# Transposing the softmax tiles of two units in every second step, with one copy out of PSUM for both and six buffers

## What is computed

```python
q = (queries @ Wq).reshape(b, s, KV_HEADS, GROUP, HEAD_DIM)   # 8 key heads x 4 query heads, 32 wide
k = (keys @ Wk).reshape(b, s, KV_HEADS, HEAD_DIM)
v = (values @ Wv).reshape(b, s, KV_HEADS, HEAD_DIM)
scores = jnp.einsum('bqhgd,bkhd->bhgqk', q, k) * scale
attn = jax.nn.softmax(scores, axis=-1)
out = jnp.einsum('bhgqk,bkhd->bqhgd', attn, v)
...
x = x + jnp.tanh(g_xattn[0]) * _L0_xattn_ref(_layernorm(x, axis=-1), ctx_4096, ctx_4096, L0_xattn_Wq, L0_xattn_Wk, L0_xattn_Wv, L0_xattn_Wo)
x = x + jnp.tanh(g_ffn[0]) * _L0_ffn_ref(_layernorm(x, axis=-1), L0_ffn_W_gate, L0_ffn_W_up, L0_ffn_W_down)
```

## Time and profile before

| | |
|---|---|
| time, median of 3 runs | 1900.26 us (1899.02 to 1903.03) |
| the profiled execution's own time | 1900.98 us |
| its span in the profile | 1899.2 us |
| PE busy | 1887.4 us (99%) |
| DVE busy | 1235.0 us (65%) |
| ACT busy | 825.8 us (43%) |
| POOL busy | 866.5 us (46%) |

### The profile page before, as it was taken

The page is one execution under the profiler, slowest core; times in us unless marked ns, Lnnn a source line. Parts: engine busy times, 40 slices in busy tenths (PEclk is TensorE's granted clock), DMA queues, the critical chain, the costliest instruction groups (busy, mean ns, idle before and its releaser), DMA issues.

```text
span 1899.2 us, 27364 instructions
## 1 busy us (share of the span) xinstructions
PE 1887.4 (99%) x9346; PEld 1555.7 (82%) x9346; DVE 1235.0 (65%) x1716; ACT 825.8 (43%) x1947; POOL 866.5 (46%) x632
## 2 busy tenths in 40 slices
PE   9999999999999999999999999999999999999999
PEld 7888888888888788888888788888888888888887
DVE  7877887787787855555554767665555555546565
ACT  5863773683584533333332444443333333333333
POOL 1430440251255598888887311116666766630000
PEclk9999999999999999999999999999999999999999
DMA  6335326326324345354536876752323232267675
GB/s 212 90 130 172 104 65 246 98 62 233 119 79 172 118 143 186 138 193 147 181 140 216 301 242 205 243 177 75 120 101 110 84 118 103 89 212 251 213 227 182
DMA packets 127196, 298.78 MB, mean 157 GB/s; under 512 B 12672, under 2 KB 24448, under 8 KB 121728
## 3 DMA queue, kind: packets, MB, share of 16 engines
q1 hardware_dynamic: 126960, 297.45, 46.3%
q10 hardware_dynamic: 144, 0.13, 0.0%
HBM read 221.25 MB, written 71.57 MB: 154 GB/s over the span
## 4 chain that ended last, share of the span: by engine, by line
PE 95%; DMA 2%; POOL 2%; DVE 1%; issue 0%; ACT 0%; SPq 0%; POOLq 0%; DVEq 0%; ACTq 0%
PE ps L1592 28%; PE ps L1594 28%; PE ps L1593 28%; PE ps L1642 3%; PE ps L1633 2%; PE ps L1653 2%; PE ps L1634 2%; PE ps L1804 1%; DMA raw<-ws 1%; PE ps L1690 1%; PE ps L1815 1%; DMA ws<-dw 1%; DMA kv_raw<-in_wc 0%; DMA dw<-in_wd 0%; DVE bl L1160 0%
## 5 line engine op out<-in xcount | busy, mean ns | idle before, releaser
L1592 PE MATMUL ps<-xop_h,w_h 128*128 128x512 f32 x1208 | 471.8, 391 | 0.0
L1594 PE MATMUL ps<-xop_h,w_l 128*128 128x512 f32 x1208 | 470.1, 389 | 0.0
L1593 PE MATMUL ps<-xop_l,w_h 128*128 128x512 f32 x1208 | 470.0, 389 | 0.0
L1160 DVE TENSOR_TENSOR bl<-raw,bh 128x1024 fp32r<-128x1024 f32 x154 | 199.5, 1304 | 143.1 <-ACT bh L862 142.8
L1594 PEld LDWEIGHTS ps<-xop_h,w_l 128*128 128x128 f32 x1208 | 226.7, 188 | 47.1
L1592 PEld LDWEIGHTS ps<-xop_h,w_h 128*128 128x128 f32 x1208 | 226.8, 188 | 46.6 <-DVE cc L1405 0.3
L1593 PEld LDWEIGHTS ps<-xop_l,w_h 128*128 128x128 f32 x1208 | 226.8, 188 | 46.4
L862 ACT ACTIVATE bh<-raw 128x1024 fp32r<-128x1024 f32 x154 | 163.0, 1061 | 225.9 <-PE ps L1594 195.9
L1160 DVE TENSOR_TENSOR w_l<-fraw,w_h 128x512 fp32r<-128x512 f32 x130 | 135.4, 1042 | 185.9 <-ACT w_h L862 185.9
L1592 PE MATMUL ps<-bh 128*128 128x512 f32 x616 | 243.0, 395 | 2.1 <-DVE bl L1160 2.0
L1594 PE MATMUL ps<-bh,bl 128*128 128x512 f32 x616 | 240.1, 390 | 0.0
(11 more groups left out here) (158 smaller groups left out, 3408.6 us busy)
## 6 DMA issues: line engine op xcount, KB each, us to landing
fraw<-in_wf SPq DMA_DIRECT2D x42, 1024.0 KB, 5.2
raw<-hs SPq DMA_DIRECT2D x154, 256.0 KB, 3.1
hs<-hsum SPq DMA_DIRECT2D x22, 1280.0 KB, 5.8
raw<-ws SPq DMA_DIRECT2D x110, 256.0 KB, 4.0
wc_raw<-in_wc SPq DMA_DIRECT2D x44, 512.0 KB, 4.6
dw<-in_wd SPq DMA_DIRECT2D x11, 1024.0 KB, 7.7
hs<-hb SPq DMA_DIRECT2D x44, 256.0 KB, 2.1
raw<-in_wd SPq DMA_DIRECT2D x44, 256.0 KB, 4.1
```

The costliest lines, as they stand in the source:

```text
L1160: return nc.vector.tensor_tensor(out, whole, hi.bitcast(F32), ALU.subtract)
L1592: pe.matmul(out, w_hi_, m_h, start=first, stop=False, skip_group_check=goes_on)
L1593: pe.matmul(out, w_hi_, m_l, start=False, stop=False, skip_group_check=goes_on)
L1594: return pe.matmul(out, w_lo_, m_h, start=False, stop=last, skip_group_check=goes_on)
```

## The change

PE transposes two units, n-4 and n-3, in every even step from 4 to 34, and none in odd steps. DVE copies both banks with one instruction of 128 x 1024 elements in each even step. So that P can wait a step longer, `pb` has six buffers of 128 x 512 in place of four (the two new ones lie in space that the loop does not use otherwise), and so have `nmx`, `sums` and `rinv`. The semaphore `pt_ready` counts pairs now.

```diff
-        pb = at("pb", [P, 4, HALF], F32, o_pb)
+        pb = [at(f"pb{n}", [P, HALF], F32, o_pb + n * 2048 if n < 4 else o_vp + (n - 4) * 2048) for n in range(PBS)]
...
             def exps(g, n):
                 act.wait_ge(maxed, g * UNITS + (n + 1))
-                if n >= 4:
-                    act.wait_ge(pt_done, g * UNITS + (n - 3))
+                if n >= PBS:
+                    act.wait_ge(pt_done, g * UNITS + (n - PBS + 1))
...
-            def pt_out(g, n):
-                m, gi = n // 2, n % 2
-                dve.wait_ge(pt_done, g * UNITS + (n + 1))
-                if n >= 8:
-                    dve.wait_ge(pv_done, g * FOURS + (n // 4 - 1))
-                nc.vector.tensor_copy(pt[:, m % 4, :, gi * P:(gi + 1) * P],
-                     ps[:, 3 + n % 2, :].rearrange("p (j q) -> p j q", j=4)).then_inc(pt_ready, 1)
+            def pt_out(g, m):
+                dve.wait_ge(pt_done, g * UNITS + (2 * m + 2))
+                if m >= 4:
+                    dve.wait_ge(pv_done, g * FOURS + (m // 2 - 1))
+                nc.vector.tensor_copy(pt[:, m % 4, :, :].rearrange("p j (g q) -> p j g q", g=2),
+                                      ps[:, 3:5, :].rearrange("p g (j q) -> p j g q", j=4)).then_inc(pt_ready, 1)
...
-                    if UNITS - 10 <= n < UNITS + 3:
-                        pt_out(g, n - 3)
+                    if UNITS - 10 <= n < UNITS + 4 and n % 2 == 0:
+                        pt_out(g, n // 2 - 2)
...
-                    if 3 <= n < UNITS - 10:
-                        pt_out(g, n - 3)
+                    if 4 <= n < UNITS - 10 and n % 2 == 0:
+                        pt_out(g, n // 2 - 2)
...
             def transpose_p(g, n):
                 pe.wait_ge(normed, g * UNITS + (n + 1))
                 if n >= 2:
-                    pe.wait_ge(pt_ready, g * UNITS + (n - 1))
+                    pe.wait_ge(pt_ready, g * (UNITS // 2) + n // 2)
...
-                    if 3 <= n < UNITS + 3:
+                    if 4 <= n < UNITS + 4 and n % 2 == 0:
+                        transpose_p(g, n - 4)
                         transpose_p(g, n - 3)
```

More of the change, by code:

```diff
@@ L35 @@
 STEPS = UNITS + 5
+PBS = 6
 COL_STEP = {5: 0, 6: 3, 7: 7, 8: 32, 9: 33}
@@ L153, in gated_cross_attention_ffn @@
         ident = small("ident", [P, P])
-        nmx = small("nmx", [P, 4, 4])
-        sums = small("sums", [P, 4, 4])
-        rinv = small("rinv", [P, 4, 4])
+        nmx = small("nmx", [P, PBS, 4])
+        sums = small("sums", [P, PBS, 4])
+        rinv = small("rinv", [P, PBS, 4])
         st = small("st", [P, 2, 12])
@@ L707, in body @@
                     pool.wait_ge(inverted, g * UNITS + (n + 1))
-                    p = pb[:, n % 4, :].rearrange("p (j k) -> p j k", j=4)
-                    r = bass.AP(rinv, (n % 4) * 4, [[16, P], [1, 4], [0, P]])
+                    p = pb[n % PBS][:, :].rearrange("p (j k) -> p j k", j=4)
+                    r = bass.AP(rinv, n % PBS * 4, [[4 * PBS, P], [1, 4], [0, P]])
                     nc.gpsimd.tensor_tensor(p, p, r, ALU.mult).then_inc(normed, 1)
@@ L907, in exps @@
                 act.wait_ge(maxed, g * UNITS + (n + 1))
-                if n >= 4:
-                    act.wait_ge(pt_done, g * UNITS + (n - 3))
+                if n >= PBS:
+                    act.wait_ge(pt_done, g * UNITS + (n - PBS + 1))
                 for j in range(4):
-                    ins = nc.scalar.activation(pb[:, n % 4, j * P:(j + 1) * P], ps[:, n % 3, j * P:(j + 1) * P],
-                                               ACT.Exp, bias=nmx[:, n % 4, j:j + 1],
-                                               accum_out=sums[:, n % 4, j:j + 1])
+                    ins = nc.scalar.activation(pb[n % PBS][:, j * P:(j + 1) * P], ps[:, n % 3, j * P:(j + 1) * P],
+                                               ACT.Exp, bias=nmx[:, n % PBS, j:j + 1],
+                                               accum_out=sums[:, n % PBS, j:j + 1])
                 ins.then_inc(exped, 1)
@@ L1210, in row_max @@
                 dve.wait_ge(s_done, g * UNITS + (n + 1))
-                nc.vector.tensor_reduce(nmx[:, n % 4, :], ps[:, n % 3, :].rearrange("p (j k) -> p j k", j=4),
+                nc.vector.tensor_reduce(nmx[:, n % PBS, :], ps[:, n % 3, :].rearrange("p (j k) -> p j k", j=4),
                                         AX_X, ALU.max, negate=True).then_inc(maxed, 1)
@@ L1215, in invert @@
                 dve.wait_ge(exped, g * UNITS + (n + 1))
-                nc.vector.reciprocal(rinv[:, n % 4, :], sums[:, n % 4, :]).then_inc(inverted, 1)
-            def pt_out(g, n):
-                m, gi = n // 2, n % 2
-                dve.wait_ge(pt_done, g * UNITS + (n + 1))
-                if n >= 8:
-                    dve.wait_ge(pv_done, g * FOURS + (n // 4 - 1))
-                nc.vector.tensor_copy(pt[:, m % 4, :, gi * P:(gi + 1) * P],
-                     ps[:, 3 + n % 2, :].rearrange("p (j q) -> p j q", j=4)).then_inc(pt_ready, 1)
+                nc.vector.reciprocal(rinv[:, n % PBS, :], sums[:, n % PBS, :]).then_inc(inverted, 1)
+            def pt_out(g, m):
[4 more added lines that the diff above has]
+                                      ps[:, 3:5, :].rearrange("p g (j q) -> p j g q", j=4)).then_inc(pt_ready, 1)
             def o_out(g, r):
@@ L1639, in transpose_p @@
                 if n >= 2:
-                    pe.wait_ge(pt_ready, g * UNITS + (n - 1))
+                    pe.wait_ge(pt_ready, g * (UNITS // 2) + n // 2)
                 for j in range(4):
-                    ins = pe.transpose(ps[:, 3 + n % 2, j * P:(j + 1) * P], pb[:, n % 4, j * P:(j + 1) * P], ident[:, :])
+                    ins = pe.transpose(ps[:, 3 + n % 2, j * P:(j + 1) * P], pb[n % PBS][:, j * P:(j + 1) * P], ident[:, :])
                 ins.then_inc(pt_done, 1)
             def weigh_values(g, r):
-                pe.wait_ge(pt_ready, g * UNITS + (4 * r + 4))
+                pe.wait_ge(pt_ready, g * (UNITS // 2) + (2 * r + 2))
                 if r >= 1:
```

## The result

The changed kernel takes 1912.39 us (median of 6 runs, 1909.94 to 1913.57), the kernel before 1900.55 (6 runs, 1899.02 to 1903.03). The ratio is 1.0057, with a 95% interval from 1.0047 to 1.0067: 9 to 13 us slower. The prediction said 1900.4 with a range from 1898.6 to 1904.2, and gave slower a chance of 0.10. It was wrong.

The account below looks back on a forecast made before the run. PE, busy 1887.4 of 1899.2 us, was taken as the bound. Stalls of 0.4 us less 0.3 for passages gave +0.1 on the profiled 1900.98, forecast as 1900.4 against the median, range 1898.6 to 1904.2.

Parts of the forecast that it names:

- The copy: DVE's 1024-element copy from PSUM: ends after 1.20 us, next instruction can start after 1.12, bank changes cost nothing.
- rival 2: Double copy is long, odd units' maxima come late behind it: 1902 us, deciding only from 1904.5; chance 0.08.
- rival 4: PE's clock falls because transposes count little as work: eight alone take 0.87 us more a pair, 1956 us; chance 0.01.
- PE's passages: On PE, 64 fewer passages from transposes back to products: a gain of 0 to 0.6 us, taken as 0.3.
- forecast sum of +0.1: Whole kernel: 0.4 us of stalls in four groups less 0.3 for passages, on the profiled 1900.98 us.
- Steps 32 and 33: PE's products there wait for exponentials of units 29 and 31: stalls of 0.07 and 0.03 us per group.
- DVE's busy time: Sign of the forecast: DVE's busy time falls by 10 us from the copies while the span stays.
- Elsewhere the waits have room.: Outside steps 32 and 33 no new stall: a pair's banks were copied a step and more earlier.
- signs of being wrong: Copy over 1.4 us, PE waiting for it, odd or even steps off 1.86 or 2.74 by over 0.03, clock leaving 1.00.
- 3 us, beside PE's work, so 0 in the sum: The 64 double copies save DVE 3 us of its queue, beside PE's work, so no gain in time.

Follow-up runs that it names:

- e1: Changed kernel with DVE waiting for the weights' high half ahead of the reciprocals, not behind them; 1900.40 us, ratio 1.0006 to the kernel before.
- e6: Changed kernel with POOL multiplying only the first 128 of the 512 columns of each P; 1901.15 us, ratio 1.0003 to the kernel before.

## Why the prediction was wrong, step by step

- **The copy** was right: 1.21 us against 1.20, no cost for the change of bank in its pattern. The 512 transposes last 0.273 us each as before, and the clock stayed at 1.00: rivals 2 and 4 did not happen.
- **PE's passages** gave nothing that shows. From the pair of step 4 to that of step 6 it takes 4.60 us in e1, and two steps of 2.30 in the kernel before are 4.60 too. The forecast of 0.3 us is under what these rows resolve. e1, which has the same pairs without the stalls, is at 1.0006 (0.9996 to 1.0015), that is 0.8 us faster to 2.9 slower: the forecast sum of +0.1 lies within, and the run can't tell it from none.
- **Steps 32 and 33** came as forecast. In step 32 of the changed kernel's first group the exponentials of unit 29 end at 124.79 and the product's weights are loaded at 124.84; the next product starts 0.30 us behind it (124.88 to 125.18), where it is 0.23 inside a step: 0.07 us, as forecast. The wait for the exponentials that the list shows, four times 0.4 us, is that of step 33. It costs PE about nothing: from the products with the values to the next instruction it is 1.01 us there (127.31 to 128.32), and in the kernel before too (124.54 to 125.55). The same 1.7 us stand in the list of e1, so they take no part in the loss.
- **DVE's busy time** was to fall by 10 us, and even in e1, without long splits, it falls by 5.5 (1235.0 to 1229.5). The forecast added up durations, and a copy of 0.68 us lets the next instruction start after 0.58. For PE this changes nothing.
- **The step that failed** is "Elsewhere the waits have room." The prediction put the wait for the banks at nothing. It was argued by the distance between the transposes, and DVE's queue was not walked there. By the rows of e1 the copy of step 4 ends 0.27 us ahead of PE's next pair, and what room is left is 0.12. The sentence that a pair's banks were copied a step and more earlier was false even without a longer split. In its place the runs show two waits for the double copy in each group, of 0.79 us in step 6 and 0.98 in step 22 by the starts, and 0.8 more behind them: 2.6 us a group, 10.4 in all. Neither place is where the distance between two pairs is shortest, which is all that the prediction looked at. PE waiting for line 1643 on `pt` is one of its own signs of being wrong.
- **The hidden assumption** behind it, and behind DVE's "3 us, beside PE's work, so 0 in the sum": that the splits keep their 1.20 us when DVE reaches them earlier. Of this pair of engines the kernel before had shown the sign. The same multiplication takes POOL 1.04 us alone and 1.93 beside a split, and step 1 of its first group has the order turned round, with the split waiting for its high half and POOL 0.44 us ahead (the rows are below). I had only its mean of 1.21 in view, as POOL had 46% to do and seemed idle enough, and did not ask who pays if the order turns.
- **The rivals**: none had this mechanism. Rival 2 has its consequence (the copy late, PE waiting for it at line 1643) by another way, and its chance was far too small for what stood in it as not walked.

Step 1 of the kernel before, on POOL and DVE, where the split takes 1.69 us in place of 1.20:

```profile
55.03 1.04 POOL L710 TENSOR_TENSOR pb<-pb,rinv 128x512 f32<-128x512 f32 x1 [13.72 <-DVE rinv L1216]
55.47 1.69 DVE L1160 TENSOR_TENSOR wc_l<-wc_raw,wc_h 128x1024 fp32r<-128x1024 f32 x1 [0.52 <-ACT wc_h L862]
```

The Trainium skill has the rule (SBUF — State Buffer, the section on the two separate sides): a VectorE instruction with two SBUF inputs and a GpSimd one that reads SBUF need the same pair of ports; the one that starts first keeps it for the whole instruction and the other is blocked. The traces agree, but for 0.11 to 0.14 us. After POOL's end at 62.97 + 1.04 = 64.01 a full split would end at 65.21, and it ended at 65.08; in e6 the same sum is 65.08 against 64.96; before, POOL's 1.04 behind the split's end at 64.44 would give 65.48, and it ended at 65.34; in step 1 of before, 55.03 + 1.04 + 1.20 = 57.27, and it ended at 57.16.

## What to carry to other kernels

Walk the queue behind every instruction whose neighbour is removed, and not only the places where a wait is known: an engine that arrives earlier can start second at a shared resource. When two engines are set off by the same event, and one instruction is much longer in some places than in others (here 1.04 and 1.93), find what is beside it, note who started first and by how much, and ask whether the change alters that order. Here a wait placed ahead of the common trigger fixes the order at no cost that shows, but the gathered transposes then bring nothing either: the work that they save lay beside PE's.

## What was unexpected in the hardware's behaviour

- The order of starts decides who pays: with the split 0.16 us ahead the two instructions take 1.19 and 1.93, with POOL 0.07 ahead 2.04 and 1.04. Together it is the same 3.1 us.
- At 0.03 us ahead by its record, POOL still lost (1.20 and 2.12), at 0.07 it won. So the recorded starts don't tell who was first when they lie as near as 0.03 us.
- Twelve reciprocals of 128 x 4 took 0.79 us of DVE's queue, 0.066 each, though a single one is recorded with 0.18.
